# Attention with experts on one core: the scale of the exponentials from registers instead of a column

## The reference

```python
cos_pm = jnp.cos(phase_modulators)          # 16 wavelengths x 16 heads
def wl_step(acc, wl):
    cpm, iw = wl
    m = cpm[None, :, None, None]
    scores = jnp.einsum('bhqd,bhkd->bhqk', Q * m, K * m) * SCALE
    scores = scores * jnp.cos(KERR * scores * scores)
    attn = jax.nn.softmax(scores, axis=-1)
    out = jnp.einsum('bhqk,bhkd->bhqd', attn, V)
    return (acc + out * iw, None)
acc, _ = jax.lax.scan(wl_step, acc0, (cos_pm, interference_weights))
```

## Time and profile before

| | |
|---|---|
| median of 3 runs | 1931.12 us (1930.82 to 1931.91) |
| the profiled execution | 1930.7 us, its span 1929.0 us |
| ACT busy | 1865.7 us, 97% of the span |
| PE busy | 1382.0 us, 72% |
| DVE busy | 775.2 us, 40% |
| POOL busy | 458.2 us, 24% |

### The profile page before, as it was taken

The page is one execution under the profiler, slowest core; times in us unless marked ns, Lnnn a source line. Parts: engine busy times, 40 slices in busy tenths (PEclk is TensorE's granted clock), DMA queues, the critical chain, the costliest instruction groups (busy, mean ns, idle before and its releaser), DMA issues. The chain is left out here.

```text
span 1929.0 us, 42815 instructions
## 1 busy us (share of the span) xinstructions
PE 1382.0 (72%) x18990; PEld 838.6 (43%) x18990; DVE 775.2 (40%) x1452; ACT 1865.7 (97%) x553; POOL 458.2 (24%) x513
## 2 busy tenths in 40 slices
PE   4786777666688888888876666666666666666665
PEld 2353444434455555555543334334344343334443
DVE  7445563333344444444433333333333333333222
ACT  3799999999999999999999999999999999999995
POOL 6122233222112122112122244433212112212111
PEclk8799999999999999999999999999999999999998
DMA  6000110000201111100000000000000000000001
GB/s 199 14 14 24 48 36 30 24 19 14 51 9 33 40 40 40 40 13 29 21 21 14 19 23 11 22 24 15 14 14 2 14 14 14 14 14 2 7 12 29
DMA packets 44985, 49.89 MB, mean 26 GB/s; under 512 B 6725, under 2 KB 37359, under 8 KB 44799
## 3 DMA queue, kind: packets, MB, share of 16 engines
q1 hardware_dynamic: 42463, 42.91, 7.2%
q0 software_dynamic: 2048, 4.20, 0.7%
q10 hardware_dynamic: 288, 0.00, 0.0%
HBM read 30.96 MB, written 15.73 MB: 24 GB/s over the span
## 5 line engine op out<-in xcount | busy, mean ns | idle before, releaser
L929 ACT ACTIVATE Pr<-T,cw 128x4096 f32<-128x4096 f32 x512 | 1843.4, 3701 | 1.1 <-DVE T L852 0.8
L894 PE MATMUL bank<-Pr,Vst 128*32 128x256 f32 x16384 | 992.5, 382 | 476.4 <-ACT Pr L929 295.2
L894 PEld LDWEIGHTS bank<-Pr,Vst 128*32 128x32 f32 x16384 | 576.9, 109 | 798.3 <-issue 616.5
L852 DVE COPY T<-bank 128x512 f32<-128x512 f32 x252 | 174.3, 692 | 504.9 <-PE bank L846 504.9
L935 POOL TENSOR_TENSOR gain<-rsum,iw_s 128x128 f32<-128x128 f32 x63 | 25.3, 402 | 1174.7 <-DVE rsum L925 1174.5
L836 DVE TENSOR_REDUCE negmax<-bank 128x2 f32<-128x512 f32 x256 | 165.1, 686 | 206.4 <-PE bank L830 205.9
L903 DVE COPY pv_s<-bank 128x512 f32<-128x512 f32 x192 | 131.4, 684 | 189.9 <-PE bank L894 189.8
L920 DVE COPY OT<-bank 128x432 f32<-128x432 f32 (+1 forms) x192 | 106.0, 552 | 121.2 <-PE bank L909 121.1
L909 PE MATMUL bank<-ident,pv_s 128*128 128x128 f32 x768 | 118.7, 277 | 24.3 <-DVE pv_s L903 24.3
L944 POOL TENSOR_TENSOR terms<-terms 128x512 f32<-128x512 f32 x126 | 128.0, 1016 | 9.9
L939 POOL TENSOR_TENSOR terms<-OT,gain 128x1024 f32<-128x1024 f32 x63 | 124.7, 1979 | 4.9
(11 more groups left out here) (168 smaller groups left out, 465.1 us busy)
## 6 DMA issues: line engine op xcount, KB each, us to landing
Ks<-qk_parts SPq DMA_DIRECT2D x31, 288.0 KB
Qs<-qk_parts SPq DMA_DIRECT2D x93, 96.0 KB
work<-in_L_ffn_w_dram SPq DMA_DIRECT2D x16, 256.0 KB, 3.8
qk_parts<-Pr SPq DMA_DIRECT2D x8, 384.0 KB, 2.8
qk_parts<-work SPq DMA_DIRECT2D x8, 384.0 KB, 2.9
dispatched<-T SPq DMA_DIRECT2D x5, 512.0 KB, 4.8
region<-dispatched SPq DMA_DIRECT2D x8, 320.0 KB, 3.7
expert_out<-work SPq DMA_DIRECT2D x8, 320.0 KB, 2.8
```

What stands on the lines that cost most here:

```text
L852: nc.vector.tensor_copy(T[par][:, ds(p * BANK, BANK)], sc_bank[rr][:, :]).then_inc(sc_read, 1)
L894: ins = nc.tensor.matmul(bank[VC * j:VC * (j + 1), half * SEQ:(half + 1) * SEQ], Vst[par][:, at:at + VC], Pr[rr][:, blk * SEQ:(blk + 1) * ...
L929: nc.scalar.activation(Pr[rr][:, :], T[par][:, :], ACT.Exp, scale=cw[:, ds(g, 1)]).then_inc(exp_done, 1)
```

## The change

A load `reg_load` fills 16 registers of ScalarE from the first partition of `cw` with the 16 scales of one unit. There are two sets of 16, used by turns. The set of unit 0 is loaded before the first exponential, the set of unit u + 1 behind the second exponential of unit u. Each exponential takes its scale from a register. The waits are the same, and so is everything on the other engines.

```diff
-            def act_step(act, g, par, rr):
-                act.wait_ge(pv_done, g + 1)
-                nc.scalar.activation(Pr[rr][:, :], T[par][:, :], ACT.Exp, scale=cw[:, ds(g, 1)]).then_inc(exp_done, 1)
+            def load_scales(act, u):
+
+                act.reg_load(scales[u % 2], cw[0:1, u * W:(u + 1) * W].bitcast(i32))
+
+            def act_step(act, u, w, par, rr):
+                act.wait_ge(pv_done, u * W + w + 1)
+                nc.scalar.activation(Pr[rr][:, :], T[par][:, :], ACT.Exp, scale=scales[u % 2][w]).then_inc(exp_done, 1)
...
+            scales = [[nc.scalar.alloc_register(f"scale{i}_{w}") for w in range(W)] for i in range(2)]
...
+                load_scales(act, 0)
...
                         for w in range(half * WH, (half + 1) * WH):
-                            act_step(act, u * W + w, par, w % 2)
+                            act_step(act, u, w, par, w % 2)
+                            if w == 1 and u + 1 < UNITS:
+                                load_scales(act, u + 1)
```

## The result

The changed kernel takes 1883.58 us (median of 4 runs, 1883.32 to 1883.79), the kernel before 1930.97 us on the same chip. The ratio is 0.9753, with a 95% interval of 0.9741 to 0.9765. The spans of the two profiled executions, 1929.0 and 1881.6 us, differ by 47.4 us; forecast were 47.1 us.

The account below looks back on a forecast made before the run. ScalarE's unbroken exponentials, 512 periods of 3.600 us, were taken to bound the kernel. 1930.7 us less 47.1 us for the column, plus 0 for the loads, gave 1883.6 us, given as 1884 us; range 1878 to 1910 us.

Parts of the forecast that it names:

- The period: ScalarE's 512 exponentials: start to start falls from 3.600 to 3.51 us without the scale column, saving 47.1 us.
- Rival 3: Exponentials: a register scale is no cheaper than the column, or overlap is lost; total about 1931 us, chance 0.06.
- My upper bound: Exponentials: saving of at most 0.10 us each from the difference of starts, 51 us in all.
- The loads: 32 register loads on ScalarE's queue: taken as 0.47 us each, hidden beside other work, adding 0 us.
- cover of 4.8 us: Time a load behind a unit's second exponential may last without delay: 1.3 us queue lead plus 3.5 us.
- My price for each register: Upper bound for a load of sixteen, if 0.468 us is paid for each register: 7.49 us.
- My break-even of 6.3 us a load: Length of each of the 31 later loads at which their excess cancels the 47.1 us saving.
- The estimate of 3.2 us: Load of sixteen at about 200 ns a register: 1.8 us exposed at the first load, total 1885.4 us.
- Rival 2: The 31 later loads wait until ScalarE is empty: about 0.6 us each, 19 us, total 1902 us; chance 0.06.
- The other engines: TensorE, VectorE and POOL keep up with a period of 3.51 us, 0.09 us less for a step.
- TensorE's least idle time: TensorE's fullest step was said to leave 0.16 us idle before the next products, 0.07 us after the change.
- One sign to look for: Exponentials on ScalarE should last about 3609 ns, with starts 3.51 us apart.

Follow-up runs that it names:

- constant: Kernel before, with the scale of all 512 exponentials as the constant 0.25 in the instruction, no column, registers or loads: 1883.78 us.
- one_by_one: Changed kernel with each set of 16 registers loaded by sixteen loads of one register, in the old place: 1893.26 us.
- twelve_loads: Changed kernel with each set loaded by 12 loads, four of two registers and eight of one, in the old place: 1887.74 us.
- singles_spread: Changed kernel with sixteen loads of one register per set, eight behind the second and eight behind the sixth exponential of the unit before: 1887.78 us.
- singles_behind_wait: Changed kernel with sixteen loads of one register per set, placed between the wait for the products and the third exponential: 2014.53 us.
- pairs: Changed kernel with each set loaded by 8 loads of two registers, in the old place: 1885.95 us.
- quads_behind_wait: Changed kernel with four loads of four registers per set, placed between the wait for the products and the third exponential: 1888.22 us.

## Why the prediction was right

**The period.** Forecast 3.51 us and 47.1 us; measured 3.507 us and 47.4 us. The pair of lines 341 and 337 in the setup, one eighth as long and of another function, gave the price: 92 ns taken, 92.3 ns measured. What carried the step was reading the starts beside the durations. Rival 3 is excluded by the period of 3.507 us itself; constant adds that a register costs no more than a number in the instruction, and the price of a column is shown with none, one and two of them. My upper bound was not quite a bound: with both differences of the starts, 0.57 and 0.48 us, off by one hundredth it would be 0.11 us (56 us), not 0.10.

**The loads.** Forecast nothing for all 32, and nothing it was. The assumed 0.47 us for a load of sixteen was the lower end and too low: it takes 1.02 us, which the cover of 4.8 us at the units and 1.4 us at the start hides as well. At the units the sum is the same for every load up to 4.8 us, so the wrong price did no harm; at the start 0.4 us were to spare. My price for each register was too dear at the other end: 7.49 us would have been 4.9 us, measured. My break-even of 6.3 us a load left out the first load's own excess; with it, it is 6.2 us. The estimate of 3.2 us by the Trainium skill's page "Runtime: NRT & Kernel Launch" (section "Instruction fetch mechanics", about 200 ns a register in bulk) is not borne out here: 1.02 us for sixteen is 64 ns a register. The loads here read SBUF; no run here shows a load from HBM.

**The cover.** The 1.3 us by which the queue goes on early, plus one period, was read off one wait's row. The load's row (121.3 us) shows the first part directly; one_by_one (0.13 us by the measured prices, 0.17 us found, 0.13 us without the four larger gaps), twelve_loads and singles_spread (none, none) show the sum, and singles_behind_wait (3.6 us expected, 3.57 us found) the first part alone. Rival 2, a load that waits for an empty engine, is excluded by the load's row at 121.3 us, in the middle of an exponential, and by the 488 exponentials without a gap.

**The other engines.** TensorE's idle time fell by what the periods lost. ScalarE waits for it once, as before, at the third exponential of unit 0, now 0.5 us in place of 0.3. One reading was wrong and did no harm: 0.16 us was not TensorE's least idle time. In the trace of before its products at 686.00 us start with no idle time at all, and this step too was on time in the changed kernel:

```profile
686.00 1.93 PE L894 MATMUL bank<-Pr,Vst 128*32 128x256 f32 x32
```

What carried this part was the 1.4 us between the end of the products and the exponential.

**One sign to look for was off.** I had said that the exponentials should last about 3609 ns. The profiled execution has 3636 ns, with the period exactly as forecast. Had I taken 65 ns from the durations, I would have found 33 us where there were 47 us.

No version of these beats the changed kernel: its period is that of constant, which has neither a column nor a load.

## What to carry to other kernels

Where one engine runs without a gap, its fixed cost for each instruction is on the path: look for operands that are given as columns although they are the same in all partitions, and price them by two instructions of the trace that differ in nothing else, start to start. Register loads on a queue that runs ahead were free here up to its lead plus one instruction; put them ahead of a wait, not behind it, and load many registers with one instruction. Before adding such work, compute the cover from the row of the queue's own wait, because the same 512 single loads cost 127 us more here in one place than in another.

## What was not expected of the hardware

**The price of a load does not grow evenly with its size.** One register takes 0.28 us, two 0.49 us, four 0.31 us, sixteen 1.02 us (medians of 512, 256, 128 and 32 loads). Why two are dearer than four I did not test.

**The recorded duration of ScalarE's instructions drifts while their period does not.** The mean is 3636 ns in the changed kernel and 3601 ns in constant, with 488 periods of 1711.76 and 1711.71 us. The first exponentials of the changed kernel's record last 3601 ns too (the row for 122.5 us above), and the median over all is 3642 ns:

```profile
L933 ACT ACTIVATE Pr<-T x512: 3599/3642/3655, 62.3 to 1855.5; 128x4096 f32<-128x4096 f32 x171
```

**A gap on ScalarE can cost TensorE its clock.** In singles_behind_wait, TensorE's idle time before its products grows to 4.61 us at unit 2's third exponential, and what follows is slower. The timeline of TensorE, and the stretches 200 to 204, 204 to 208 and 208 to 212 us, whose third number from the right is the granted clock:

```profile
196.03 1.94 PE L894 MATMUL bank<-Pr,Vst 128*32 128x256 f32 x32 [0.21 <-ACT Pr L936]
...
203.11 3.64 PE L894 MATMUL bank<-Pr,Vst 128*32 128x256 f32 x32 [4.61 <-ACT Pr L936]
...
207.55 1.93 PE L894 MATMUL bank<-Pr,Vst 128*32 128x256 f32 x32
```

```profile
200.00:204.00 4.00, 0.89 (x12) 0.51 (x16) 0.69 (x2) 4.00 (x2) 1.72 (x1) 0.57 0.36 115
204.00:208.00 4.00, 4.00 (x40) 1.78 (x36) 0.67 (x2) 3.67 (x2) 0.96 (x1) 0.58 0.02 4
208.00:212.00 4.00, 3.89 (x64) 2.55 (x60) 3.31 (x9) 4.00 (x2) 0.00 (x0) 1.00 0.05 16
```

TensorE is idle from 198.5 to 203.1 us. In the first two stretches its clock stands at the lower of its two levels (1.2 of 2.4 GHz) for most of the time, in the third it is back. The same 32 matmuls take 3.64 us instead of 1.93 us and end too late for the exponential that reuses their buffer: 12.4 us of ScalarE's idle time is put down to such products. One of these 29 waits, 3.47 us at 319.90 us, is the loads' own gap by its place and length; 8.9 us in 28 waits remain, and each also loses the overlap of 0.10 us. The mean clock over the span is 0.945 in this run, and 0.987 in the changed kernel.

The gap of pairs at 301.82 us comes about in the same way without a gap of ScalarE ahead of it. TensorE's timeline, and its clock in 300 to 302 us:

```profile
298.03 0.61 PE L830 MATMUL bank<-Ks,Qs 72*128 72x256 bf16 x4 [1.78 <-DMA Qs<-qk_parts]
298.57 3.20 PE L894 MATMUL bank<-Pr,Vst 128*32 128x256 f32 x32
```

```profile
300.00:302.00 2.00, 2.00 (x22) 0.70 (x14) 0.00 (x0) 1.42 (x2) 1.69 (x4) 0.50 0.00 0
```

TensorE waits 1.78 us for a transfer, the clock falls to the lower level, the products take 3.20 us, and ScalarE waits 0.58 us for them. quads_behind_wait has the same at 300.68 us (0.79 us). In twelve_loads TensorE waits 2.28 us at this place and keeps the upper level (products 1.93 us). So the wait just before does not tell alone whether the clock falls; what does is not settled here.
